# First attention: the causal mask moves from a TensorE matmul into VectorE's row maximum, and the exponentials read on-chip memory

## What is computed

```python
qkv = hidden_states @ Wqkv_w.T + Wqkv_b          # 16 query heads, 8 key heads of 128, values of 256
def attn_map(qi, ki):
    s = einsum('bqhd,bkhd->bhqk', qi, ki) * scale
    s = where(causal, s, finfo(float32).min)
    return softmax(s, axis=-1)
p = attn_map(q[..., 0, :], k[..., 0, :]) - lam * attn_map(q[..., 1, :], k[..., 1, :])
o = einsum('bhqk,bkhe->bqhe', p, v)               # then an RMS norm and the output projection
```

## Time and profile before

| | |
|---|---|
| runs, us | 1629.63, 1631.5, 1633.35 |
| span of the profiled execution, us | 1649.7 |
| granted TensorE clock, mean | 0.994 |
| first attention, batch 0 | about 28 to 443 us |
| first attention, batch 1 | about 842 to 1260 us |
| TensorE matmul busy | 1550.0 us (94%) |
| VectorE busy | 1101.0 us (67%) |
| ScalarE busy | 930.4 us (56%) |
| GpSimd busy | 636.6 us (39%) |

### The profile page before, as it was taken

How to read it: one execution, slowest core, us unless ns; L and a number is a source line. 1 busy time by engine, 2 the same in 40 slices (tenths; PEclk the granted TensorE clock), 3 DMA queues, 4 the chain that set the end, 5 groups by cost and what they waited for, 6 DMA issues and landing times.

```text
span 1649.7 us, 30985 instructions
## 1 busy us (share of the span) xinstructions
PE 1550.0 (94%) x10774; PEld 1341.8 (81%) x10774; DVE 1101.0 (67%) x2705; ACT 930.4 (56%) x2054; POOL 636.6 (39%) x582
## 2 busy tenths in 40 slices
PE   8999999999899999999898999999998999998985
PEld 7888889888888677688787898898988876776885
DVE  6767667677645787574577676676766377874655
ACT  5666565665444577543556655656654346775353
POOL 1635444554461101252535354444654510031631
PEclk9999999999999999999999999999999999999998
DMA  3110000020120422034220200000201113322132
GB/s 132 46 52 17 27 1 16 25 91 1 40 69 10 75 51 61 21 120 137 76 96 1 77 18 26 16 7 18 91 1 58 50 36 61 60 60 101 56 126 106
DMA packets 48195, 88.03 MB, mean 53 GB/s; under 512 B 9600, under 2 KB 30480, under 8 KB 46928
## 3 DMA queue, kind: packets, MB, share of 16 engines
q1 hardware_dynamic: 43552, 75.28, 15.9%
q0 software_dynamic: 3744, 10.26, 1.7%
q10 hardware_dynamic: 768, 0.79, 0.2%
HBM read 60.18 MB, written 19.76 MB: 48 GB/s over the span
## 4 chain that ended last, share of the span: by engine, by line
PE 66%; DVE 15%; ACT 9%; issue 6%; POOL 3%; ACTq 1%; DMA 0%; DVEq 0%; POOLq 0%; SPq 0%
PE ps L408 16%; PE ps L410 15%; PE ps L409 15%; PE ps L1193 4%; PE ps L1210 4%; PE ps L1153 4%; ACT E L1407 3%; DVE nmax L1806 3%; PE ps L916 2%; POOL E L2274 2%; ACT PT_h L1389 1%; DVE On L1724 1%; DVE PT_l L1781 1%; PE ps L1189 1%; PE ps L844 1%
## 5 line engine op out<-in xcount | busy, mean ns | idle before, releaser
L1407 ACT ACTIVATE E<-ps,nmax 128x128 f32<-128x128 f32 (+7 forms) x256 | 188.9, 741 | 208.5 <-DVE nmax L1806 208.2
L2271 POOL TENSOR_SCALAR E<-E,mixc 128x128 f32<-128x128 f32 (+7 forms) x128 | 97.0, 758 | 396.2 <-DVE mixc L1774 396.2
L1806 DVE TENSOR_REDUCE nmax<-ps 128x1 f32<-128x128 f32 (+7 forms) x256 | 183.3, 749 | 12.7 <-PE ps L893 12.5
L1568 ACT ACTIVATE PT<-ps 128x512 f32<-128x512 f32 x288 | 155.0, 601 | 58.8 <-PE ps L1193 57.7
L2274 POOL TENSOR_TENSOR E<-E 128x128 f32<-128x128 f32 (+7 forms) x128 | 182.4, 1425 | 10.7
L408 PE MATMUL ps<-V_h,PT_h 128*128 128x256 f32 x576 | 168.0, 292 | 0.5 <-DVE O L1786 0.5
L409 PE MATMUL ps<-V_l,PT_h 128*128 128x256 f32 x576 | 163.8, 284 | 0.0
L410 PE MATMUL ps<-V_h,PT_l 128*128 128x256 f32 x576 | 163.6, 284 | 0.0
L408 PE MATMUL ps<-K_h,Q_h 128*128 128x512 f32 (+3 forms) x384 | 147.4, 384 | 8.7 <-ACT E L1407 5.4
L2026 DVE CUSTOM_DVE_ANT_0 masked<-ps,causal 128x128 bf16<-128x128 f32 (+3 forms) x256 | 111.1, 487 | 39.5 <-PE ps L1153 37.8
L1781 DVE TENSOR_TENSOR PT_l<-ps,PT_h 128x128 fp32r<-128x128 f32 (+7 forms) x128 | 96.7, 756 | 60.7 <-ACT PT_h L1389 60.0
(11 more groups left out here) (265 smaller groups left out, 4622.8 us busy)
## 6 DMA issues: line engine op xcount, KB each, us to landing
Wa_raw<-in_wa SPq DMA_DIRECT2D x8, 1024.0 KB, 6.0
Fw_raw<-in_fa SPq DMA_DIRECT2D x32, 256.0 KB, 2.6
E_raw<-in_fe SPq DMA_DIRECT2D x8, 768.0 KB, 7.5
xs<-in_xs SPq DMA_DIRECT2D x2, 2967.0 KB, 12.6
Wo_raw<-in_wo SPq DMA_DIRECT2D x8, 512.0 KB, 3.5
yg<-ys SPq DMA_DIRECT2D x8, 512.0 KB, 5.2
xg<-xs SPq DMA_DIRECT2D x6, 645.0 KB, 8.1
KS<-QK_h SPq DMA_DIRECT2D x56, 64.0 KB
```

The source lines that it names most:

```text
L1407: nc.scalar.activation(e[:, 0:w], ps[m][:, 0:w], ACT.Exp, bias=nmax[:, s % 4, m:m + 1], accum_out=lsum[:, s % 4, m:m + 1]).then_inc(exp_do ...
L1568: nc.scalar.activation(PT[:, at:at + HALF], bank1(RING1 + n % RING1), ACT.Exp, scale=SCALE1).then_inc(t_used, 1)
L1806: nc.vector.tensor_reduce(nmax[:, s % 4, m:m + 1], ps[m][:, 0:(q_tile(s, last) + 1) * P], AX.X, ALU.max, negate=True).then_inc(nmax_ready[ ...
```

## The change

The mask matmul goes. VectorE's maximum becomes a tensor_tensor_reduce: it reads the scores out of PSUM and the bf16 mask `causal` out of SBUF, writes the negated masked scores as float32 into E1 or E2, and gives the negated maximum. The exponential then reads that SBUF tile and writes over it, with scale -1. `scores(s)` waits for `nmax_ready` instead of `exp_done`. A map wider than 512 is given as two halves, for which the mask is read with overlapping rows; `causal` grows by 128 columns (640) and is built at the start by VectorE. The wait in front of the new instruction stands alone, followed by a nop. To make room, `ident` becomes a view of `ident_r`, and `sq_junk` becomes bf16.

```diff
@@ program
+CAUSAL = HALF + P
-    ident = sb("ident", [P, P])
+    ident = ident_r[:].bitcast(F32)
+    causal = sb("causal", [P, CAUSAL], BF16)
-        sq_junk = sb("sq_junk", [P, E0], F32, s)
+        sq_junk = sb("sq_junk", [P, E0], BF16, s)
+            ident_raw = sb("ident_raw", [P, P], F32, r)
-    causal = sb("causal", [P, HALF], BF16, s)
-    FILLS = 9
+    FILLS = 7
@@ tensor: scores(n)
-                        pe.wait_ge(exp_done[m], STEPS0 * it + n)
+                        pe.wait_ge(nmax_ready[m], STEPS0 * it + n)
...
-                    mm = nc.tensor.matmul(ps[m][:, tile(i)], ident_r[:], mask_r[:],
-                                          start=False, stop=True, skip_group_check=True)
@@ tensor: tail of a group
-                        pe.wait_ge(exp_done[n // 2], STEPS0 * it + STEPS0)
+                        pe.wait_ge(nmax_ready[n // 2], STEPS0 * it + STEPS0)
@@ scalar
-                    nc.scalar.activation(e[:, 0:w], ps[m][:, 0:w], ACT.Exp, bias=nmax[:, s % 4, m:m + 1],
+                    nc.scalar.activation(e[:, 0:w], e[:, 0:w], ACT.Exp, scale=-1.0, bias=nmax[:, s % 4, m:m + 1],
@@ vector
+        def mask_parts(scores, negated, w):
+
+            if w <= HALF:
+                return scores[:, 0:w], negated[:, 0:w], causal[:, CAUSAL - w:]
+            zeros = causal[:, HALF - w // 2:HALF]
+            added = bass.AP(zeros.tensor, zeros.offset, [list(zeros.ap[0]), [P, 2], [1, w // 2]])
+            return *(a[:, 0:w].rearrange("p (c n) -> p c n", c=2) for a in (scores, negated)), added
...
-                for m in range(2):
+                for m, e in ((0, E1[s % 2]), (1, E2[s % 2])):
                     dve.wait_ge(s_ready[m], STEPS0 * it + s + 1)
-                    nc.vector.tensor_reduce(nmax[:, s % 4, m:m + 1], ps[m][:, 0:(q_tile(s, last) + 1) * P], AX.X, ALU.max,
-                                            negate=True).then_inc(nmax_ready[m], 1)
+                    dve.nop(nofuse=True)
+                    scores, negated, added = mask_parts(ps[m], e, (q_tile(s, last) + 1) * P)
+                    nc.vector.tensor_tensor_reduce(out=negated, in0=scores, in1=added, scale=-1.0, scalar=3e38, op0=ALU.add,
+                                                   op1=ALU.min, accum_out=nmax[:, s % 4, m:m + 1]).then_inc(nmax_ready[m], 1)
@@ vector: lambdas(), at the start
+            nc.vector.memset(causal[:, 0:HALF], 0.0)
+            nc.vector.tensor_copy(causal[:, HALF:], mask_raw[:])
@@ gpsimd, once per batch
-            nc.gpsimd.memset(causal[:, 0:HALF - P], 0.0).then_inc(filled, 1)
-            nc.gpsimd.tensor_copy(causal[:, HALF - P:], mask_r[:].bitcast(F32)).then_inc(filled, 1)
```

More of the change, by code:

```diff
@@ L715, in _ @@
         load_x_half(0, 0)
-        sp.dma_start(ident[:], d["ident"]).then_inc(ident_in, 16)
+        sp.dma_start(ident_raw[:], d["ident"]).then_inc(ident_in, 16)
         load_x_half(0, 1)
@@ L808, in transpose_x @@
                         mm = nc.tensor.transpose(x_bank(k, j)[:, c * 2 * P + r * P:c * 2 * P + (r + 1) * P],
-                                                 (X if k else Xn)[:, 2 * j + r, tile(c)], ident[:])
+                                                 (X if k else Xn)[:, 2 * j + r, tile(c)], ident[:] if b or k else ident_raw[:])
                 mm.then_inc(xt_ps, 1)
@@ L2026, in row_max @@
                     ins = nc.vector.tensor_tensor_reduce(out=masked[:, j % RING1, cols], in0=scores,
-                                                         in1=causal[:, HALF - (z - a):], scale=-1.0, scalar=3e38, op0=ALU.add,
+                                                         in1=causal[:, CAUSAL - (z - a):], scale=-1.0, scalar=3e38, op0=ALU.add,
                                                          op1=ALU.min, accum_out=dst)
@@ L2186, in _ @@
         dve.wait_ge(ident_in, 16)
-        nc.vector.tensor_copy(ident_r[:], ident[:]).then_inc(pre_dve, 1)
+        nc.vector.tensor_copy(ident_r[:], ident_raw[:]).then_inc(pre_dve, 1)
         x_parts(0, 0, 0)
```

## The result

The kernel after the change takes 1635.9 us (median of 12 runs, 1632.9 to 1637.5), the kernel before on the same chip 1632.3 us (median of 12): ratio 1.0019, 95% interval [1.0011, 1.0027], that is 3.1 us slower, where 1623 was forecast. Its profiled execution took 1637.2 us for a span of 1635.4.

The account below looks back on a forecast made before the run. The chain was taken to alternate between TensorE stretches and ScalarE/VectorE loops. Terms -13.2 - 4.1 + 2.0 + 1.2 + 1.5 + 0.4 = -12.2 us, less 3.8 for GpSimd's path, gave -8.4: 1623 us, range 1607 to 1635.

Parts of the forecast that it names:

- The mask matmuls: TensorE, first attention: 256 matmuls removed at 0.12 us each, 110 of them on the chain, -13.2 us.
- the second path: Weight turns waiting for GpSimd behind a TensorE stretch: four mask matmuls per group go to it, taking 3.8 us off the gain.
- The wait for the exponential: Next scores wait for the maximum alone: 0.43 us saved at 8 group starts plus one 0.67 us, -4.1 us.
- The exponential out of SBUF: ScalarE reads SBUF in place of PSUM: 0.037 us more for each of 54 exponentials on the chain, +2.0 us.
- The form: VectorE's maximum as tensor_tensor_reduce: 0.02 us more for each of 59 maxima on the chain, +1.2 us.
- Wait and nop: Maxima waiting for TensorE start 0.10 us later, about 15 on the chain, +1.5 us; nothing behind another VectorE instruction.
- The rival of the instruction's start: Wait and nop before each VectorE maximum not covered, accumulator read not hidden: slower, about 1634 to 1637 us; chance 15%.
- The constants: VectorE sets zeros and casts 128 columns during batch 0's projections, delaying the last Q_l on the chain, +0.4 us.
- The loops take it all: ScalarE and VectorE steps lengthen, TensorE gains only at group starts and a third of its stretches: 1629 us, no change; 18%.

Follow-up runs that it names:

- the shifted kernel: The changed kernel plus 32 long-met waits, each on a nop, in VectorE's program between the batches: 0.9981 of the kernel before.
- before': The kernel before, unchanged, in a second trace used for the comparisons: span 1630.7 us, run of 1632.5 us.
- e1: The kernel before without the 256 mask matmuls and nothing else: ratio 0.9973, -4.4 us.
- e13: The changed kernel with 118 long-met waits on nops in VectorE's program between the batches: ratio 1.0078.
- e12: The changed kernel with one wait and one nop a step, the first maximum waiting for both maps' scores: ratio 1.0118, 19 us slower.
- e11: The changed kernel without the nop in the two groups of each batch outside the loop (128 of 256 maxima): ratio 0.9988.
- e14: The changed kernel with 64 long-met waits on nops in VectorE's program between the batches: ratio 1.0027.

## Why the prediction was wrong

- **The mask matmuls, -13.2 us, or -9.4 behind the second path**: mis-sized, this is the step that failed. Measured -4.3 (groups of after) and -4.4 (alone; 5.0 by its groups). The 0.12 us a piece was right (0.23 between passes across the border), the number of pieces was not: 110 lay on the chain that ended last, but only about four of a group's 16 steps got shorter, and these by 0.11 to 0.20 us of 0.24. TensorE's longer waits name what came next, some 0.1 us behind: GpSimd's weights and the splits of the output projection's input. I had taken this off for four matmuls a group and left the rest at full price.
- **The wait for the exponential, -4.1**: failed. The groups show 0.9 us, two thirds of it from the one wait of 0.67 us. Elsewhere the 0.43 us of TensorE idle on the chain went, and the next maximum began at the same time, since VectorE was not free. I had named only the maximum as late next, not the bias additions and the mix in front of it.
- **The exponential out of SBUF, +2.0**: right in the price (38 ns between starts for 37), wrong in the count: 5.1 us in the groups (2.9 in the runs) for 54 x 0.037. "VectorE: DVE Perf Modes" of the Trainium skill, section "The TRN2 errata", has 52 cycles more for ScalarE's SBUF source than for its PSUM source, 43 ns at its 1.2 GHz. The rows of the exponentials grew by 31 ns only, but the distance between starts by 43 in the median of 231 (38 in the mean), so the trace agrees with that rule in direction and in size.
- **The form, +1.2**: 0.43 us in three groups, 1.1 in eight. Right.
- **Wait and nop, +1.5**: its size in the steps is right (0.23 us in three groups, 0.6 in eight, and 0.1 at each border). What failed is that "behind another VectorE instruction it costs nothing" looked only at when an instruction starts. The nops made the loop's code longer, and where it now lies in batch 1, packets of code come again in the second turn and VectorE stands: +4.7 us in the trace of after. No term and no rival of mine had this. The rival of the instruction's start ended near the right time (1634 to 1637) for a wrong reason.
- **The constants, +0.4**: not seen; the first exponential begins at 29.39 us in the shifted kernel and 29.56 in before', and between 28.3 and 29.8 in all traces.
- **The rivals.** "The loops take it all" named what holds: a third of TensorE's stretches, the longer exponential in most steps. Its mechanism holds, its single terms don't: it took the full 4.1 us for the wait. It gave 1629 us, or 0.9985 of the kernel before; the shifted kernel, which is this change without the stalls, measures 0.9981. That the two are so close is in part luck, since the groups explain only a part of the 3.1 us.

In sum by the parts, for eight groups: -4.3 - 0.9 + 5.1 + 1.1 + 0.6 = +1.6, borders -0.7 (six times 28.07 against 28.18), stalls +4.7: +5.6 us. The spans of after and before' differ by 4.7, the runs by 3.1 [1.8, 4.4]. Read off the two traces directly, the 4.7 us are: first exponential -1.1, first groups +1.0 (batch 0, with a fall of the clock, below) and -1.0 (batch 1), the six other groups +1.5 without the stalls, borders -0.8 without them, stalls +4.7, the rest +0.4. So the parts hold for the groups behind the first ones. The first groups go by the clock as well, and between traces and runs some 2 us stay open.

## What to carry to other kernels

A chain shows where time is, not what it is worth: before a saving on it is booked, ask for each step which instruction is next in line and when its engine is free. An addition to the engine that closes a loop step by step is paid by half or more (0.64 of 1.2 us a group for the exponential, 9.3 of 9.9 for the maximum's start); a saving on an engine that runs a little ahead of it is worth less than it looks (4.4 of 13.2 us for the mask matmuls on the chain). And an edit that adds instructions to a long loop should be timed again with a few dozen harmless ones in front of it: here 32 turned a loss of 3 us into a gain of 3.

## What the runs showed of the hardware

- **Code loading on VectorE, by place.** With 235 instructions in the loop's body (before, before', e1) the second turn needs no packet of queue 14. With 267 and 299 it needs none in batch 0 and, in batch 1, 3 or 4 of 8 KB in the first microseconds, with VectorE idle for 2.3 to 2.6 us and then for 1.4 to 1.9 us (0.5 in e13). Moving the loop by +32, +64, -64 (e12) or -95 instructions (e11) ends it, +118 brings it back. This fits a period of 128 instructions. Other rules may fit as well: before' executed 3,354 instructions of VectorE on 54 packets, some 60 a packet. How the code is held near the engine stays open.
- **The clock behind a wait.** TensorE's falls to the lower level were not the same from trace to trace at the same code. After, then the shifted kernel, whose program is the same up to here, 60 to 66 us:

```profile
60.00:66.00 6.00, 4.20 (x26) 4.09 (x25) 2.30 (x9) 3.86 (x9) 4.55 (x5) 0.74 0.01 3
```

```profile
60.00:66.00 6.00, 4.24 (x37) 4.13 (x37) 2.29 (x8) 4.19 (x10) 5.03 (x5) 1.00 0.01 3
```

Both wait 1.8 us for GpSimd there; one group has steps of 69.25 us, the other of 67.93. One such fall costs 1.3 us, nearly half of the 3.1 us by which the program got slower. The change has its part in it. With the mask matmul the wait is 1.1 to 1.3 us, and none of the eight traces with that matmul has a fall in batch 0's first group. In the seven traces of the changed kernel and its variants without the matmul it is 1.7 to 2.0 us, and three of them have a fall behind it (after, e11, e14).
- **Waits in a row.** Many long-met waits on a nop are not free: from 64 to 118 of them in a row the idle time of VectorE grew by 10.3 - 7.4 = 2.9 us, 0.05 us each, while those in front of the maxima added 0.23 us in three groups (96 of them).
